# Four-layer graph network on one core: the convolutions' running sums as a tree, the ranking's running sums by pairs of tiles

## The chip, the cores and the metric

One core of one Trainium2 chip. The time is device microseconds of one execution of the whole program (three executions of the kernel before are given, and one profiled execution). Engines are named as in the profile: PE (TensorE; PEld its weight loads), DVE (VectorE), ACT (ScalarE), POOL (GpSimd), SP (SyncE).

## What is computed

12,500 nodes with 64 features, 200,000 edges sorted by their target `dst`. Four layers run in turn, each added to x and normalised per row:

```python
out0 = segment_sum(exp(-w)[:, None] * x[dst], src)            # sums by the edge's source
h1   = [seg_sum, seg_max, seg_mean](edge_attr_32, src), u     # then a two-layer MLP
conv: h = x @ W; out = segment_sum(h[src] * norm, dst) + b    # twice (c1, c2)
attention: softmax of scores over the edges of one dst, out = segment_sum(h[src] * attn, dst)
x = layernorm(x + layer(x))                                   # after each layer
```

What matters here is the segment sum over sorted edges. The kernel makes it as a running sum: state[t] = same_dst[t] * state[t-1] + row[t], where same_dst[t] is 1 if edge t has the target of edge t-1 and 0 otherwise. The state at a node's last edge is its sum.

## The kernel before, in words

The edges are padded to 128 partitions of L = 1568 consecutive edges. One "tile" is one edge of each partition (128 rows), and J = 16 tiles make a block; there are NBLK = 98 blocks. The program has these stages, one after the other.

1. *Preparation and histograms*: ids to digits, one-hot matrices (L1055, L1056), counts on PE.
2. *Ranking*: every edge's place in an order by source is worked out, and a row (message, edge attributes, id) is written there. DVE works block by block: `stage_a(n, q)` does four tiles of block n, each with one step of the running sum of node rows (L1110, into `xb`, which waits by the semaphore v_tiles for the step before) and one rank count (L1112, accumulating into `rank_blk`); `stage_b(n-1, q)` does four selections from PSUM for the block before (L1125, waits for "counted" from PE). Four such rounds make a block; then `positions(n-1)` (L1136, L1137) makes the indices, and `onehots_of(n+1)` (L1092, L1093) the next one-hots. PE makes histograms (L841) and counts (L850), ACT copies and scales rows (L753, behind v_tiles), POOL writes the 16 tiles of a block to HBM by 16 indirect DMAs (L591), behind `positions` of that block.
3. *Source pass*: running sums and maxima over rows sorted by source (L1215, L1220), no gathers.
4. *Dense parts* of a layer: transposes and products on PE, norms on DVE.
5. *Convolution* `conv(g)`, twice (c1 and c2): POOL gathers a block's 16 tiles from a table in HBM by 16 indirect DMAs (L641) into one of four buffers `gb`; it may start block n when DVE has finished block n-4. DVE makes the running sum over the 16 tiles of a block, one instruction for each (L1495), each waiting by the semaphore "chain" for the one before. SP writes the block's states to HBM (L507).
6. *Attention* ("at"): the same gathers, of 68 columns. Its running sum is a tree already: `sums_of` (`join`, L1425) takes 33 instructions per block with waits at the levels alone, and ten more DVE instructions per block deal with the scores. The products of same_dst over 2, 4 and 8 tiles that the tree needs stand in `run`, which lies in the buffers of the digits hi_dst, lo_dst and hi_src and is made ahead of conv("c1") (L1526, L1528).

After each pass POOL fetches the states at the nodes' last edges (L610).

Of the kernel before, what the change touches and what calls it, by code (L numbers as in the profile page):

```python
# [15 lines left out]
P = 128  # L16
# [3 lines left out]
J = 16  # L20
Q = 4
NB = -(-N_EDGES // (P * 2 * J))
L = NB * 2 * J
# [32 lines left out]
    "onehots": 2 * NB, "onehots_used": 2 * NB, "flag": 1, "flagrow": 1, "chain": (J - 1) * NBLK,  # L56
# [91 lines left out]
def program(nc, a, out):  # L148
    with ExitStack() as ctx:
# [104 lines left out]
        def carve(tensor, parts, dt=f32):  # L254

            at, got = 0, {}
            for name, size in parts:
# [7 lines left out]
                              ("junk", (2 + Q) * P // 2), ("hi0", J * P // 2), ("hi1", J * P // 2)])  # L265
# [6 lines left out]
        junk = [cut["junk"].bitcast(bf16)[:, q * P:(q + 1) * P] for q in range(2 + Q)]  # L272
# [27 lines left out]
        def one(onehot, k):  # L300
# [14 lines left out]
               for level, (o, w) in ((1, ("dst", "hi")), (2, ("dst", "lo")), (3, ("src", "hi")))}  # L315
        a16 = [late[f"a16_{h}"] for h in range(2)]
# [396 lines left out]
        def _(act):  # L713
# [29 lines left out]
            for n in range(NBLK):  # L743
# [218 lines left out]
        def _(v):  # L962
# [134 lines left out]
            onehots_of(0)  # L1097
            v.wait_ge(s("decay_ready"), 1)
# [3 lines left out]
            def stage_a(n, q):  # L1102

                h = n % 2
                for k in range(q * Q, (q + 1) * Q):
                    t = n * J + k
                    old = xb[h][:, k - 1, :] if k else xb[1 - h][:, J - 1, :] if n else first_row[:, :]
                    if t:
                        v.wait_ge(s("v_tiles"), t)
                    v.scalar_tensor_tensor(out=xb[h][:, k, :], in0=old, scalar=same_dst[:, t:t + 1],  # L1110
                                           in1=xs[h][:, k, :], op0=ALU.mult, op1=ALU.add).then_inc(s("v_tiles"), 1)
                    rank = v.scalar_tensor_tensor(out=junk[t % 2], in0=ids_in[h][:, k * P:(k + 1) * P],  # L1112
                                                  scalar=src_f[:, t:t + 1], in1=before[:, :],
                                                  op0=ALU.is_equal, op1=ALU.mult, accum_out=rank_blk[:, h, k:k + 1])
                if q == J // Q - 1:
                    rank.then_inc(s("ranked"), 1)

            def stage_b(n, q):

                v.wait_ge(s("counted"), n * (J // Q) + q + 1)  # L1120
                h, group = n % 2, n * (J // Q) + q
                if group:
                    v.wait_ge(s("selected"), group)
# [594 lines left out]
```

## Time and profile before

| | us |
|---|---|
| median of 3 executions | 11174.61 (11172.26 to 11193.84) |
| the profiled execution | 11183.53 |
| its span, first to last instruction | 11181.7 |
| ranking, about 490 to 2885 | 2395 |
| convolution c1, gathers and sums, 3850 to 6043 | 2193 |
| convolution c2, gathers and sums, 6223 to 8415 | 2192 |
| attention, 8707 to 10990 | 2283 |

Of the span, POOL is busy 64%, DVE 42%, PE 16%, ACT 10%. A row of the trace gives for a group of instructions its busy time, the mean of one in ns, then "|" and the idle time of its engine just before them, with what ended that idle time: another engine's instruction, a DMA, "issue" (nothing that the profile shows) or "remote" (a releaser that it doesn't know).

### The profile page before, as it was taken

To read this page: it belongs to the slowest core of one execution; us is meant where nothing else is said; L and a number is where in the kernel's file an instruction comes from. 1 tells how busy PE (TensorE), PEld (TensorE's weight loads), DVE (VectorE), ACT (ScalarE), POOL (GpSimd) and SP (SyncE) were. 2 spreads that over 40 slices of the span, in tenths; PEclk is the share of its full clock that TensorE was granted. 3 is DMA by queue.
4 is the path that set the end of the run, shared out by engine and by line. 5 is a ranking of instruction groups with operands and counts; after the bars stand their busy time and mean duration, and the time that the engine had idled before them with its cause. 6 is when DMAs were issued, how large, how long until landed. Compare 5 with 4: busy or idle time off the path is not lost.

```text
span 11181.7 us, 57120 instructions
## 1 busy us (share of the span) xinstructions
PE 1801.6 (16%) x9285; PEld 1516.5 (14%) x9285; DVE 4736.9 (42%) x20005; ACT 1142.1 (10%) x2728; POOL 7106.9 (64%) x6884
## 2 busy tenths in 40 slices
PE   8744444444000400000000000000001000000000
PEld 7633333333000300000000000000000000000000
DVE  8855555555797422222221222222224344444446
ACT  0143434343000100000000000000000000000000
POOL 0566666666201377777776677777777776666766
PEclk7755555555555555555555555555555555555555
DMA  5144444444575111111111111111111222222221
GB/s 224 57 129 122 129 124 126 124 127 122 204 273 203 32 50 46 48 46 48 46 48 37 50 46 48 46 48 46 48 46 30 54 53 58 53 58 55 56 55 44
DMA packets 570444, 911.29 MB, mean 81 GB/s; under 512 B 333435, under 2 KB 348228, under 8 KB 544824
## 3 DMA queue, kind: packets, MB, share of 16 engines
q1 hardware_dynamic: 350264, 652.74, 17.3%
q0 software_dynamic: 219904, 255.88, 10.8%
q14 instruction: 226, 1.85, 0.1%
q8 instruction: 50, 0.82, 0.0%
HBM read 494.12 MB, written 414.02 MB: 81 GB/s over the span
## 4 chain that ended last, share of the span: by engine, by line
DVE 34%; issue 28%; another core or an unknown queue 17%; POOL 16%; PE 3%; DMA 1%; ACT 1%; DVEq 0%; SPq 0%; POOLq 0%; ACTq 0%
DVE arena_a L1495 16%; POOL arena_a L641 15%; DVE arena_b L1112 4%; DVE arena_a L1110 3%; DVE arena_b L1125 3%; DVE arena_a L1425 3%; POOL arena_a L610 2%; PE bank L811 2%; DVE arena_b L1056 1%; DVE arena_b L1093 1%; PE bank L916 1%; DVE arena_a L1625 0%; PE bank L890 0%; DMA arena_a<-in_a 0%
## 5 line engine op out<-in xcount | busy, mean ns | idle before, releaser
L641 POOL DMA_INDIRECT arena_a<-table_c,decay x3136 | 3284.6, 1047 | 1257.6 <-issue 1051.2
L1495 DVE SCALAR_TENSOR_TENSOR arena_a<-arena_a,same_dst 128x64 f32<-128x64 f32 x3134 | 891.5, 284 | 3449.5 <-DVE arena_a L1495 2713.2
L591 POOL DMA_INDIRECT by_src<-arena_b,idx_blk x1568 | 1570.8, 1002 | 885.8 <-issue 449.4
L641 POOL DMA_INDIRECT arena_a<-table_at,decay x1568 | 1556.8, 993 | 703.8 <-issue 468.4
L1110 DVE SCALAR_TENSOR_TENSOR arena_a<-arena_a,same_dst 128x64 f32<-128x64 f32 x1567 | 441.9, 282 | 711.1 <-remote 547.7
L864 PE MATMUL bank<-ident,chunk_end 128*64 128x128 f32 (+2 forms) x8 | 2.7, 442 | 4416.0 <-DVEq L973 4416.0
L864 PEld LDWEIGHTS bank<-ident,chunk_end 128*64 128x64 f32 (+2 forms) x8 | 1.4, 240 | 4416.6 <-DVEq L973 4416.6
L1112 DVE SCALAR_TENSOR_TENSOR arena_b<-arena_a,src_f,before 128x128 bf16<-128x128 f32 x1568 | 543.7, 347 | 37.4 <-issue 37.4
L850 PE MATMUL bank<-hrows 98*128 98x128 f32 x1568 | 404.0, 440 | 659.5 <-DVE arena_b L1125 331.9
L850 PE MATMUL bank<-hrows,arena_a 98*128 98x128 f32 x1568 | 403.3, 438 | 658.0 <-DVE arena_b L1125 347.4
L753 ACT ACTIVATE arena_b<-arena_a,decay 128x64 f32<-128x64 f32 x1568 | 394.2, 334 | 972.5 <-remote 610.2
L1215 DVE SCALAR_TENSOR_TENSOR arena_a<-arena_a,mask_blk,hrows 128x96 f32<-128x96 f32 x1567 | 489.5, 312 | 7.4 <-DVE arena_a L1220 4.4
L850 PEld LDWEIGHTS bank<-hrows 98*128 98x128 f32 x1568 | 348.7, 327 | 711.6 <-DVE arena_b L1125 313.8
L850 PEld LDWEIGHTS bank<-hrows,arena_a 98*128 98x128 f32 x1568 | 347.3, 326 | 710.6 <-DVE arena_b L1125 329.6
L1125 DVE SCALAR_TENSOR_TENSOR arena_b<-bank,arena_b 128x128 bf16<-128x128 f32 x1568 | 380.7, 287 | 107.9 <-issue 107.1
L599 POOL DMA_INDIRECT fix_rows<-states_src,fix_from_src x1 | 1.0, 957 | 668.3 <-DMA states_src<-arena_a 668.3
L811 PE MATMUL bank<-arena_b 128*98 128x128 bf16 x3136 | 406.5, 299 | 26.9 <-DVE arena_b L1056 24.9
L943 PE MATMUL bank<-ident,arena_a 128*128 128x128 f32 x196 | 67.4, 447 | 2124.3 <-DMA arena_a<-in_a 1141.4
L1220 DVE SCALAR_TENSOR_TENSOR arena_a<-arena_a,cap_blk,hrows 128x32 f32<-128x32 f32 x1567 | 384.8, 246 | 0.0
L811 PEld LDWEIGHTS bank<-arena_b 128*98 128x98 bf16 x3136 | 365.0, 174 | 68.9 <-DVE arena_b L1056 68.6
L571 POOL DMA_INDIRECT x_at_start<-x,start_i x98 | 143.4, 1464 | 276.3 <-DVEq L973 246.7
L943 PEld LDWEIGHTS bank<-ident,arena_a 128*128 128x128 f32 x196 | 28.7, 205 | 2137.2 <-DMA arena_a<-in_a 1148.7
(279 smaller groups left out, 4845.9 us busy)
## 6 DMA issues: line engine op xcount, KB each, us to landing
arena_a<-ids_rows SPq DMA_DIRECT2D x98, 1024.0 KB
states_src<-arena_a SPq DMA_DIRECT2D x98, 1024.0 KB
states_c<-arena_a SPq DMA_DIRECT2D x196, 512.0 KB
hrows<-by_src SPq DMA_DIRECT2D x98, 776.0 KB, 6.1
states_at<-arena_a SPq DMA_DIRECT2D x98, 576.0 KB
x_at_start<-arena_a SPq DMA_DIRECT2D x7, 7168.0 KB, 49.0
arena_a<-x_at_start SPq DMA_DIRECT2D x98, 512.0 KB
arena_a<-table_c,decay POOLq DMA_INDIRECT x3136
```

Of the source, the lines that this page charges most:

```text
L591: pool.indirect_dma_start(out=by_src, out_offset=AT(ap=idx_blk[r][:, k:k + 1], axis=0), in_=rows[r][:, k, :], in_offset=None)\
L641: pool.indirect_dma_start(out=gb[r][:, k * w:(k + 1) * w], out_offset=None, in_=table[g], in_offset=AT(ap=src_i[:, n * J + k:n * J + k + 1 ...
L753: ins = act.activation(rows[n % R][:, k, 0:D], xb[n % 2][:, k, :], ACT.Copy, scale=decay[:, t:t + 1])
L811: last = pe.matmul(hist[k % streams], one(oh_hi[h], k), one(oh_lo[h], k), start=False, stop=False)
L850: last = pe.matmul(p_cnt[q][:, k % Q * P:(k % Q + 1) * P], hi_t[h][:, at], snap[h][:, at], start=True, stop=True)
L1110: v.scalar_tensor_tensor(out=xb[h][:, k, :], in0=old, scalar=same_dst[:, t:t + 1], in1=xs[h][:, k, :], op0=ALU.mult, op1=ALU.add).then_inc ...
L1112: rank = v.scalar_tensor_tensor(out=junk[t % 2], in0=ids_in[h][:, k * P:(k + 1) * P], scalar=src_f[:, t:t + 1], in1=before[:, :], op0=ALU. ...
L1125: chosen = v.scalar_tensor_tensor(out=junk[2 + k % Q], in0=p_cnt[q][:, k % Q * P:(k % Q + 1) * P], scalar=1.0, in1=one(oh_lo[h], k), op0=A ...
L1215: xk = c2.done(v.scalar_tensor_tensor(out=new[:, 0:WS], in0=old[:, 0:WS], scalar=mask_blk[:, q, k:k + 1], in1=tb[h][:, k, 0:WS], op0=ALU.m ...
L1220: ins = v.scalar_tensor_tensor(out=new[:, WS:W01], in0=old[:, WS:W01], scalar=cap_blk[:, q, k:k + 1], in1=tb[h][:, k, D:WS], op0=ALU.min, ...
L1425: return v.scalar_tensor_tensor(out=made[:, k, :], in0=old, scalar=scalar, in1=raw[:, k, :] if first else made[:, k, :], op0=ALU.mult, op1 ...
L1495: ins = v.scalar_tensor_tensor(out=st[h][:, k * D:(k + 1) * D], in0=old, scalar=same_dst[:, e:e + 1], in1=gb[r][:, k * D:(k + 1) * D], op0 ...
```

## The change

Three parts.

*Convolution.* The block's running sum becomes the tree of the attention stage, without its halves: `join(0)` from the carried state, seven joins of raw pairs (k = 3, 5, ..., 15), `join(1)`, then for spans 2, 4 and 8 eight joins each. One semaphore increment stands at the end of each level. That is 33 instructions in place of 16.

*Ranking.* The running sum goes by pairs of tiles: `pair_alone` adds the first tile of a pair to the second; `pair_joined` adds the carried state to the second, by the product `both_same` of the pair's two masks, and then to the first. That is 24 instructions per block in place of 16. Two selections of the block before, and then two rank counts, stand between one pair and the next. ACT waits for pairs (v_pairs). Two more scratch rows ("junk") are there.

*Once*: `both_same` is made by one DVE multiplication, in the buffer hi_dst.

```diff
+    "onehots": 2 * NB, "onehots_used": 2 * NB, "flag": 1, "flagrow": 1, "chain": 4 * NBLK,
...
+        both_same = digits["dst", "hi"][:, :].bitcast(f32)[:, 0:L // 2]
...
-                        act.wait_ge(s("v_tiles"), t + Q)
+                        act.wait_ge(s("v_pairs"), (t + Q) // 2)
...
+            link(v.tensor_tensor(both_same, masks[:, :, 0], masks[:, :, 1], ALU.mult))
...
+            def pair_alone(n, i):
+                h, t = n % 2, n * J + 2 * i
+                ins = v.scalar_tensor_tensor(out=xb[h][:, 2 * i + 1, :], in0=xs[h][:, 2 * i, :],
+                                             scalar=same_dst[:, t + 1:t + 2], in1=xs[h][:, 2 * i + 1, :],
+                                             op0=ALU.mult, op1=ALU.add)
+                if i == 0:
+                    ins.then_inc(s("pair_begun"), 1)
+            def pair_joined(n, i):
+                h, t, pair = n % 2, n * J + 2 * i, n * (J // 2) + i
+                old = xb[h][:, 2 * i - 1, :] if i else xb[1 - h][:, J - 1, :] if n else first_row[:, :]
+                if pair:
+                    v.wait_ge(s("v_pairs"), pair)
+                v.scalar_tensor_tensor(out=xb[h][:, 2 * i + 1, :], in0=old, scalar=both_same[:, pair:pair + 1],
+                                       in1=xb[h][:, 2 * i + 1, :], op0=ALU.mult, op1=ALU.add)
+                v.scalar_tensor_tensor(out=xb[h][:, 2 * i, :], in0=old, scalar=same_dst[:, t:t + 1],
+                                       in1=xs[h][:, 2 * i, :], op0=ALU.mult, op1=ALU.add).then_inc(s("v_pairs"), 1)
...
-                for q in range(J // Q):
+                if n < NBLK:
+                    pair_alone(n, 0)
+                for i in range(J // 2):
+                    if n < NBLK and i + 1 < J // 2:
+                        pair_alone(n, i + 1)
+                    if n:
+                        select(n - 1, 2 * i)
+                        select(n - 1, 2 * i + 1)
                     if n < NBLK:
-                        stage_a(n, q)
-                    if n:
-                        stage_b(n - 1, q)
+                        if i == 0:
+                            v.wait_ge(s("pair_begun"), n + 1)
+                        pair_joined(n, i)
+                        rank_of(n, 2 * i)
+                        rank_of(n, 2 * i + 1)
...
-                    for k in range(J):
-                        if k:
-                            old = st[h][:, (k - 1) * D:k * D]
-                            v.wait_ge(s("chain"), chained)
...
+                    join(0, carried, same_dst[:, e:e + 1], raw[:, 0, :])
+                    for k in range(3, J, 2):
+                        last = join(k, raw[:, k - 1, :], same_dst[:, e + k:e + k + 1], raw[:, k, :])
+                    last.then_inc(s("chain"), 1)
+                    chained += 1
+                    v.wait_ge(s("chain"), chained)
+                    join(1, made[:, 0, :], same_dst[:, e + 1:e + 2], raw[:, 1, :]).then_inc(s("chain"), 1)
+                    chained += 1
+                    for span, product in run.items():
+                        v.wait_ge(s("chain"), chained)
+                        for k in range(J):
+                            if k // span % 2:
+                                last = join(k, made[:, k // span * span - 1, :],
+                                            product[:, n, k // (2 * span) * span + k % span:][:, 0:1],
+                                            raw[:, k, :] if k % span == 0 else made[:, k, :])
+                        if 2 * span < J:
+                            last.then_inc(s("chain"), 1)
                             chained += 1
+                    last.then_inc(s("state"), 1)
```

On DVE, one block of a convolution was this before (same_dst is the mask, arena_a the buffers and the states):

```order
L1495 SCALAR_TENSOR_TENSOR arena_a<-arena_a,same_dst 128x64 [waits gathered2,state,stored0]
L1495 SCALAR_TENSOR_TENSOR arena_a<-arena_a,same_dst 128x64 [waits chain] x15
```

and is this now (hi_dst, lo_dst and hi_src hold the products over 2, 4 and 8 tiles):

```order
L1519 SCALAR_TENSOR_TENSOR arena_a<-arena_a,same_dst 128x64 [waits gathered2,state,stored0]
L1519 SCALAR_TENSOR_TENSOR arena_a<-arena_a,same_dst 128x64 x7
L1519 SCALAR_TENSOR_TENSOR arena_a<-arena_a,same_dst 128x64 [waits chain]
L1519 SCALAR_TENSOR_TENSOR arena_a<-arena_a,hi_dst 128x64 [waits chain]
L1519 SCALAR_TENSOR_TENSOR arena_a<-arena_a,hi_dst 128x64 x7
L1519 SCALAR_TENSOR_TENSOR arena_a<-arena_a,lo_dst 128x64 [waits chain]
L1519 SCALAR_TENSOR_TENSOR arena_a<-arena_a,lo_dst 128x64 x7
L1519 SCALAR_TENSOR_TENSOR arena_a<-arena_a,hi_src 128x64 [waits chain]
L1519 SCALAR_TENSOR_TENSOR arena_a<-arena_a,hi_src 128x64 x7
```

Fifteen waits on "chain" became four, and 16 instructions 33. On DVE in the ranking, a round of four tiles was this before, four times in a block:

```order
L1110 SCALAR_TENSOR_TENSOR arena_a<-arena_a,same_dst 128x64 [waits v_tiles]
L1112 SCALAR_TENSOR_TENSOR arena_b,rank_blk<-arena_a,src_f,before 128x128
L1110 SCALAR_TENSOR_TENSOR arena_a<-arena_a,same_dst 128x64 [waits v_tiles]
L1112 SCALAR_TENSOR_TENSOR arena_b,rank_blk<-arena_a,src_f,before 128x128
L1125 SCALAR_TENSOR_TENSOR arena_b,sel_blk<-bank,arena_b 128x128 [waits selected,counted]
L1125 SCALAR_TENSOR_TENSOR arena_b,sel_blk<-bank,arena_b 128x128 x3
```

(of the four tiles, two stand here), and four tiles are this now:

```order
L1108 SCALAR_TENSOR_TENSOR arena_a<-arena_a,same_dst 128x64
L1141 SCALAR_TENSOR_TENSOR arena_b,sel_blk<-bank,arena_b 128x128 x2
L1120 SCALAR_TENSOR_TENSOR arena_a<-arena_a,hi_dst 128x64 [waits v_pairs]
L1122 SCALAR_TENSOR_TENSOR arena_a<-arena_a,same_dst 128x64
L1128 SCALAR_TENSOR_TENSOR arena_b,rank_blk<-arena_a,src_f,before 128x128 x2
L1108 SCALAR_TENSOR_TENSOR arena_a<-arena_a,same_dst 128x64
L1141 SCALAR_TENSOR_TENSOR arena_b,sel_blk<-bank,arena_b 128x128 [waits selected,counted]
L1141 SCALAR_TENSOR_TENSOR arena_b,sel_blk<-bank,arena_b 128x128
L1120 SCALAR_TENSOR_TENSOR arena_a<-arena_a,hi_dst 128x64 [waits v_pairs]
L1122 SCALAR_TENSOR_TENSOR arena_a<-arena_a,same_dst 128x64
L1128 SCALAR_TENSOR_TENSOR arena_b,rank_blk<-arena_a,src_f,before 128x128 x2
```

With the two instructions of `positions` and the two of `onehots_of`, a block of the ranking had 52 DVE instructions and has 60. Nothing is moved on PE, ACT, POOL or SP.

## Rows read from the trace of the kernel before

**Rows 1.** Busy time by stretch: ranking, c1, attention (stretch, us, PE, PEld, DVE, ACT, POOL)
```profile
490.00:2885.00 2395.00, 1012.35 (x4704) 879.05 (x4704) 1368.43 (x8238) 968.91 (x2158) 1570.83 (x1568) 0.50 0.42 124
3850.00:6070.00 2220.00, 1.37 (x4) 0.79 (x4) 451.06 (x1583) 0.00 (x0) 1658.15 (x1585) 0.50 0.18 47
...
8707.00:10990.00 2283.00, 173.26 (x596) 120.63 (x596) 1000.10 (x4235) 98.77 (x395) 1557.78 (x1569) 0.50 0.24 57
```
**Rows 2.** Groups by line in c1, 3860 to 6044
```profile
L641 POOL DMA_INDIRECT arena_a<-table_c,decay x1560 | 1634.7, 1048 | 523.7 <-issue 523.7
L1495 DVE SCALAR_TENSOR_TENSOR arena_a<-arena_a,same_dst 128x64 f32<-128x64 f32 x1567 | 445.7, 284 | 1725.0 <-DVE arena_a L1495 1363.0 <-remote 158.5 <-issue 108.6
```
**Rows 3.** Timeline of the start of c1 (start us, us, engine line)
```profile
3850.06 1.03 POOL L641 DMA_INDIRECT arena_a<-table_c,decay  x1 [158.94 <-DMA table_c<-hrows]
...
3871.78 4.78 DVE L1495 SCALAR_TENSOR_TENSOR arena_a<-arena_a,same_dst 128x64 f32<-128x64 f32 x15
...
3891.59 5.10 DVE L1495 SCALAR_TENSOR_TENSOR arena_a<-arena_a,same_dst 128x64 f32<-128x64 f32 x16 [15.03 <-DMA arena_a<-table_c,decay]
...
3893.96 0.98 POOL L641 DMA_INDIRECT arena_a<-table_c,decay  x1 [0.30 <-issue]
```
**Rows 4.** Timeline in the middle of c1
```profile
5000.09 1.10 POOL L641 DMA_INDIRECT arena_a<-table_c,decay  x1 [0.30 <-issue]
5000.50 0.28 DVE L1495 SCALAR_TENSOR_TENSOR arena_a<-arena_a,same_dst 128x64 f32<-128x64 f32 x1 [1.11 <-DVE arena_a L1495]
5001.49 1.09 POOL L641 DMA_INDIRECT arena_a<-table_c,decay  x1 [0.30 <-issue]
5001.90 0.28 DVE L1495 SCALAR_TENSOR_TENSOR arena_a<-arena_a,same_dst 128x64 f32<-128x64 f32 x1 [1.12 <-DVE arena_a L1495]
```
**Rows 5.** Timeline of the end of c1
```profile
6017.27 1.09 POOL L641 DMA_INDIRECT arena_a<-table_c,decay  x1 [0.30 <-issue]
...
6041.48 0.28 DVE L1495 SCALAR_TENSOR_TENSOR arena_a<-arena_a,same_dst 128x64 f32<-128x64 f32 x1 [1.81 <-remote]
6042.18 0.28 DVE L1495 SCALAR_TENSOR_TENSOR arena_a<-arena_a,same_dst 128x64 f32<-128x64 f32 x1 [0.41 <-DVE arena_a L1495]
```
**Rows 6.** Group of the gathers in the attention stage
```profile
L641 POOL DMA_INDIRECT arena_a<-table_at,decay x1568 | 1556.8, 993 | 703.8 <-issue 468.4 <-DVE arena_a L1425 160.6 <-remote 74.8
```
**Rows 7.** Timeline in the attention stage
```profile
9458.07 0.29 DVE L1425 SCALAR_TENSOR_TENSOR arena_a<-arena_a,hi_dst 128x68 f32<-128x68 f32 x1 [1.57 <-issue]
...
9459.47 0.29 DVE L1425 SCALAR_TENSOR_TENSOR arena_a<-arena_a,hi_dst 128x68 f32<-128x68 f32 x1 [1.11 <-issue]
...
9465.40 0.94 POOL L641 DMA_INDIRECT arena_a<-table_at,decay  x1 [0.30 <-issue]
...
9468.62 0.97 DVE L1425 SCALAR_TENSOR_TENSOR arena_a<-arena_a,lo_dst 128x68 f32<-128x68 f32 x4 [2.53 <-remote]
...
9473.94 0.94 POOL L641 DMA_INDIRECT arena_a<-table_at,decay  x1 [7.59 <-DVE arena_a L1425]
```
**Rows 8.** Timeline of a block of the ranking
```profile
1600.87 1.44 POOL L591 DMA_INDIRECT by_src<-arena_b,idx_blk  x1 [3.62 <-DVE idx_blk L1137]
...
1602.53 0.28 DVE L1110 SCALAR_TENSOR_TENSOR arena_a<-arena_a,same_dst 128x64 f32<-128x64 f32 x1
...
1603.00 0.28 DVE L1110 SCALAR_TENSOR_TENSOR arena_a<-arena_a,same_dst 128x64 f32<-128x64 f32 x1
...
1619.09 0.28 DVE L1110 SCALAR_TENSOR_TENSOR arena_a<-arena_a,same_dst 128x64 f32<-128x64 f32 x1 [2.26 <-remote]
...
1620.51 0.95 POOL L591 DMA_INDIRECT by_src<-arena_b,idx_blk  x1 [0.30 <-issue]
1621.88 0.28 DVE L1110 SCALAR_TENSOR_TENSOR arena_a<-arena_a,same_dst 128x64 f32<-128x64 f32 x1 [2.24 <-remote]
...
1625.04 1.44 POOL L591 DMA_INDIRECT by_src<-arena_b,idx_blk  x1 [3.58 <-DVE idx_blk L1137]
```
**Rows 9.** What POOL waits for in the ranking, 536 to 2885 (us in total, times, longest)
```profile
POOL by_src L591 <- DVE idx_blk L1137: 350.4, 96, 5.1
```

More of the change, by code:

```diff
@@ L271, in program @@
         rows = [cut[f"rows{r}"].rearrange("p (j f) -> p j f", f=TW) for r in range(R)]
[L272 removed]
+        junk = [cut["junk"].bitcast(bf16)[:, q * P:(q + 1) * P] for q in range(4 + Q)]
         hi_in = [cut[f"hi{h}"].bitcast(bf16)[0:HIGH, :] for h in range(2)]
@@ L1097, in _ @@
             onehots_of(0)
+            masks = same_dst[:, :].rearrange("p (m two) -> p m two", two=2)
+            link(v.tensor_tensor(both_same, masks[:, :, 0], masks[:, :, 1], ALU.mult))
             v.wait_ge(s("decay_ready"), 1)
             v.wait_ge(s("first_row_in"), 16)
[L1102 to L1115, printed above, removed]
-                    rank.then_inc(s("ranked"), 1)
@@ L1118, in stage_b @@
[L1118 to L1123, printed above, removed]
-                for k in range(q * Q, (q + 1) * Q):
-                    chosen = v.scalar_tensor_tensor(out=junk[2 + k % Q], in0=p_cnt[q][:, k % Q * P:(k % Q + 1) * P],
-                                                    scalar=1.0, in1=one(oh_lo[h], k), op0=ALU.mult, op1=ALU.mult,
-                                                    accum_out=sel_blk[:, h, k:k + 1])
-                chosen.then_inc(s("selected"), 1)
+            def pair_alone(n, i):
[5 more added lines that the diff above has]
+                    ins.then_inc(s("pair_begun"), 1)
@@ new lines, in rank_of, with select @@
+            def rank_of(n, k):
+                h, t = n % 2, n * J + k
+                rank = v.scalar_tensor_tensor(out=junk[2 + Q + k % 2 if k % 4 > 1 else k % 2], in0=ids_in[h][:, k * P:(k + 1) * P],
+                                              scalar=src_f[:, t:t + 1], in1=before[:, :],
+                                              op0=ALU.is_equal, op1=ALU.mult, accum_out=rank_blk[:, h, k:k + 1])
+                if k == J - 1:
+                    rank.then_inc(s("ranked"), 1)
+            def select(n, k):
+                q, h, group = k // Q, n % 2, n * (J // Q) + k // Q
+                if k % Q == 0:
+                    v.wait_ge(s("counted"), group + 1)
+                    if group:
+                        v.wait_ge(s("selected"), group)
+                chosen = v.scalar_tensor_tensor(out=junk[2 + k % Q], in0=p_cnt[q][:, k % Q * P:(k % Q + 1) * P],
+                                                scalar=1.0, in1=one(oh_lo[h], k), op0=ALU.mult, op1=ALU.mult,
+                                                accum_out=sel_blk[:, h, k:k + 1])
+                if k % Q == Q - 1:
+                    chosen.then_inc(s("selected"), 1)
@@ new lines, in conv, with join @@
+                    made = st[h][:, 0:J * D].rearrange("p (j c) -> p j c", c=D)
+                    carried = chunk_end[:, 0:D] if n == 0 else st[1 - h][:, (J - 1) * D:J * D]
+                    e = n * J
+                    def join(k, old, scalar, new):
+                        return v.scalar_tensor_tensor(out=made[:, k, :], in0=old, scalar=scalar, in1=new,
+                                                      op0=ALU.mult, op1=ALU.add)
+                    join(0, carried, same_dst[:, e:e + 1], raw[:, 0, :])
```

16 lines of the change are left out of this document (2 added, 14 removed).

## The prediction, on record before the changed kernel's times were seen

> **What bounds the kernel now.** First the busy time by stretch: the two convolutions take 2192 us each (c1 from 3850.06 to 6042.46 [rows 3, 5], c2 as long), the ranking 2395, attention 2283, and in all of them POOL is the busiest engine, with 1560 to 1660 us, though nowhere full [rows 1]. So the question in each is what keeps POOL from its pace. That pace is a gather of 0.94 us and 0.30 us of issue, 1.25 us together, 20.0 us for the 16 of a block, seen in attention beside DVE's work [rows 7] and in c1's first blocks, which start 20 us apart [rows 3].
>
> In c1 the groups by line show that POOL never waits for DVE there (all its idle time is "issue"), yet its mean gather is 1.05 us [rows 2]. The timeline says how: at first DVE does the 16 steps of a block in 5.1 us, 0.32 us a step, chain waits included, and then idles 15 us for the gathers [rows 3]. In the middle of c1 the same step comes every 1.40 us, and POOL's gathers, now 1.09 us long, also every 1.40 us, in lockstep [rows 4]: 16 x 1.40 = 22.4 us a block. The rows say that 1.11 us of each step is a wait for the step before. The first blocks deny it: the same wait cost 0.04 us there. And in attention, joins that wait for nothing also come 1.40 us apart, with no named releaser [rows 7]. So I read the 1.40 us as a **slow mode of DVE, priced per instruction**, not as the latency of a semaphore.
>
> When is DVE slow? In attention POOL's last gather before a stall ends at 9466.34; at 9468.62 DVE does four joins in 0.97 us, finishes, and frees the buffer at which POOL starts again at 9473.94 [rows 7]. In the ranking POOL stands still 3.6 us in each block, then DVE does a tile in 0.47 us, and later in the block, with POOL writing, in 2.8 us, two instructions at 1.40 [rows 8]. In both a standstill of POOL buys DVE a stretch of fast work. c1's end speaks against too simple a rule: POOL's last gather ends at 6018.36 and DVE still makes two steps in 2.8 us at 6042 [rows 5], after 2168 us in which POOL never stood.
>
> **Prices.** I count DVE's instructions per block (attention 43, ranking 52, convolution 16) and give 1 per 1.40 us to the time in which POOL works. Attention: a block is 2283 / 98 = 23.3 us, of it POOL waits (160.6 + 74.8) / 98 = 2.4 us for DVE [rows 1, 6]. In the other 20.9 us go 14.9 instructions, so 28.1 are bought by 2.4 us: 11.7 per us of standstill. Ranking: a block is 24.2 us (1600.87 to 1625.04 [rows 8]), POOL waits 350.4 / 96 = 3.65 us [rows 9], 14.7 go in the other 20.6 us and 37.3 are bought: 10.2 per us. Two stages with different work give nearly the same price; that is why I trust it.
>
> **The convolutions.** 15 waits become 4, and 16 instructions 33. By this reading the waits are worth nothing and the 17 instructions are the cost. What is gained is another thing: with 33 instructions DVE falls behind, POOL runs into its four buffers, stands, and the lockstep breaks as in attention. POOL's gathers then cost 20.0 us a block plus something for DVE's work beside them. Attention's mean of 993 ns would give 16 x (0.993 + 0.30) = 20.7, but it holds a 1.2 us product that c1 lacks; c1's own first blocks, with DVE's steps beside the gather, show 0.98 at most [rows 3], so 20.1. In it go 14.4 instructions; 18.6 remain, at 11.7 to 10.2 per us 1.6 to 1.8 us. Several blocks' debt is paid in one longer stall, so I take 1.5. A block is 21.6 us. For c1: 98 x 21.6 = 2117 for POOL, and a tail of 12 us for DVE's last block (24 before, in slow mode [rows 5]; 7 if all fast): 2129 against 2192, **-63 us, for both -126**. Bounds of the block: 20.1 (no stall; -210 each) and attention's whole 23.3 (+103 each).
>
> One rule of the Trainium skill bears on the step: "VectorE: DVE Perf Modes", Rules for kernel authors, says to minimise the number of operations and not of semaphores, since each operation drains anyway. By that rule the tree, with twice the instructions and fewer waits, brings nothing of itself; the trace agrees (0.32 us with the wait, at first [rows 3], against 0.20 to 0.25 for a join without one [rows 7]), and it speaks against this change.
>
> **The ranking.** The running sum goes from 16 to 24 instructions, a block from 52 to 60. The waits on v_tiles go, but in the fast stretch the tile of 0.47 us is just the two instructions back to back [rows 8], so their going is worth 0. Of the order nothing else is on a path: ACT scales after pairs as it did after tiles, POOL waits for `positions` at the end of the block as before, SP's next loads wait for the last rank count, now the block's last sum, and are wanted a block later. PE's counts for a group wait for the same selections. So 8 instructions more, in front of `positions`, for which POOL waits. At 10.2 per us: 0.8 us a block, +77. Least: DVE is still slow 0.4 us after POOL's last write ended (1621.88 against 1621.46), so all 37 were bought in a good us, and 8 more cost 0.2 us, +20. Most: all 8 behind each other at 0.20 us in POOL's standstill, 1.6 us, +157. I take 0.5, **+50 us**. `both_same` once is under 1 us. The attention stage, the dense parts and the source pass are left as they are: 0.
>
> **Sum.** -126 + 50 = -76 us against the profiled execution's 11183.5, that is 11107; the median of the runs lies 9 us lower, so 11098, say **11100 us**.
>
> **Rivals.**
> *A. The convolutions become like attention or worse (slower).* The mechanism: in slow mode 33 instructions last 46 us against POOL's 20, and if the standstills don't buy DVE a fast stretch soon enough, POOL waits longer than the lockstep cost. For: attention, the same tree on the same gathers, takes 23.3 us a block, more than c1's 22.1 (2168 / 98); and the end of c1, where DVE stayed slow for 24 us without POOL [rows 5]. Against: attention has ten instructions more. It decides from a block of 22.1 us, that is a stall over 2.0 us. At 23.3: 98 x 23.3 + 12 = 2295, +103 each; with the ranking +256, **11430**. Were POOL's gathers to stay at 1.40 us as well, 22.4 + 1.5 = 23.9 would give the same and a little more. Chance 0.20.
> *B. The slow mode is the wait after all, and POOL is the bound.* Then the tree hides: 33 joins of 0.20 us are 7 us, a block is 20.1, 98 x 20.1 + 10 = 1980, -212 each, -374 with the ranking, **10800**. For: the releaser named in rows 2 and 4. Against: rows 3 and 7. Chance 0.13.
> The skill's "Runtime: NRT & Kernel Launch", Instruction fetch mechanics, holds that the supply of instructions is hidden behind their issue; by that rule no price per instruction of 1.40 us could exist, and B would hold. The joins of rows 7, without waits, speak against it; no run so far shows what the 1.40 us is.
> *C. The two parts cancel.* The ranking at its upper price (+157) and the convolutions at 21.5 to 21.6 (-126 to -140): about **11190**. Chance 0.12.
> *D. POOL keeps 1.40 us by itself, whatever DVE does*, its stalls hidden: convolutions as before, ranking +50: **11225**. Against: the early blocks of c1. Chance 0.06.
>
> **Chances.** The forecast, with a gain of 20 to 200 us, has 0.49. A measurement here tells 0.2%, 22 us, from no change. Faster by more: most of the forecast (0.47) and B (0.13), 0.60. Same: C, and the rest of the forecast, 0.14. Slower: A and D, 0.26. The range must hold 0.8: it leaves out B's end and the far half of A: 10870 to 11330. The forecast alone would span 10980 to 11160.
>
> **What would show it.** In c1 after: POOL's mean gather near 0.95 to 0.99 us in place of 1.05, and, new, waits of POOL for the join line, some 150 us in all per convolution, in about 20 stalls of 5 to 10 us; blocks of DVE in 7 us right after a stall and in 40 us and more later; a mean block of 21.6. In the ranking: POOL's wait for the indices 4.1 us a block in place of 3.65, and the v_pairs waits empty. Wrong it would be if POOL waits for nothing and its gathers are 0.94 (B), if its stalls sum to over 200 us per convolution (A), or if the ranking's block grows by over 1 us, or shrinks: a shorter block with 8 more instructions would refute the price per instruction.

## The result, and the profile after

| | before | changed |
|---|---|---|
| median of the runs | 11182.24 us (4) | 11364.18 us (4, 11356.18 to 11385.17) |
| ratio | | 1.0162, 95% interval 1.0145 to 1.0180 |
| span of the profiled execution | 11181.7 us | 11362.8 us |

The change is slower by 182 us, where a gain of 76 was forecast. The busy time by stretch of the changed kernel (ranking, c1, attention; columns: us, PE, PEld, DVE, ACT, POOL), to be read beside [rows 1]:

```profile
490.00:2991.00 2501.00, 1013.98 (x4706) 879.58 (x4704) 1561.11 (x9022) 981.59 (x2158) 1564.17 (x1568) 0.50 0.41 119
3959.00:6190.00 2231.00, 1.37 (x4) 0.79 (x4) 687.60 (x3250) 0.00 (x0) 1498.35 (x1571) 0.50 0.18 46
...
8870.00:11130.00 2260.00, 169.25 (x582) 117.67 (x582) 964.01 (x4081) 96.58 (x385) 1565.33 (x1574) 0.50 0.23 56
```

POOL's 1568 gathers or scatters mark each stage in the same way in both traces, so I measure a stage from the start of the first to the end of the last of them; the tables below all do.

| POOL's stage | before | changed | difference |
|---|---|---|---|
| up to the first scatter | 511.8 | 516.5 | +5 |
| ranking | 2370.6 | 2474.5 | +104 |
| to the first gather of c1 | 967.6 | 968.6 | +1 |
| c1 | 2168.3 | 2205.2 | +37 |
| between | 204.3 | 195.4 | -9 |
| c2 | 2167.8 | 2199.0 | +31 |
| between | 316.7 | 318.4 | +2 |
| attention, and the rest | 2474.5 | 2485.3 | +11 |

Up to rounding they add up to the 181 us between the spans. The attention stage was not changed, and it and the rest took 2476.6 to 2488.7 us in four other kernels at the same level of time (those of the table below), so the 11 us lie within its scatter. What is to be explained is the ranking's +104 and the convolutions' +68.

The group of the gathers in c1, 3959 to 6190 (busy, mean ns | idle time before, releasers), and what POOL waits for in the ranking (us in total, times, longest):

```profile
L642 POOL DMA_INDIRECT arena_a<-table_c,decay x1568 | 1496.1, 954 | 867.8 <-issue 471.6 <-DMA table_c<-hrows 158.8 <-remote 121.0
```
```profile
POOL by_src L592 <- DVE idx_blk L1154: 458.6, 95, 5.5
```

Beside [rows 2] the mean gather went from 1048 to 954 ns, so the lockstep is gone, as forecast. But new waits took more than it had cost: POOL stands 22 times in c1 for over 2.5 us, 235 us in all, and a cycle of five blocks is 112.5 us nearly throughout. In the ranking the wait for the indices went from 3.65 us a block [rows 9] to 4.83.

The timeline of a slow stretch of c1 in the changed kernel (start us, us, engine line):

```profile
4395.77 1.69 DVE L1519 SCALAR_TENSOR_TENSOR arena_a<-arena_a,lo_dst 128x64 f32<-128x64 f32 x8 [8.85 <-remote]
4396.02 0.95 POOL L642 DMA_INDIRECT arena_a<-table_c,decay  x1 [0.30 <-issue]
...
4406.97 1.26 DVE L1519 SCALAR_TENSOR_TENSOR arena_a<-arena_a,hi_src 128x64 f32<-128x64 f32 x6 [9.51 <-remote]
```

Here the 1.40 us shows a face that the kernel before could not show. VectorE runs the eight joins of a level back to back in 1.69 us. Then the wait for the last of them takes 9.5 us, so levels start 11.20 us apart, and that is 8 x 1.40. So within a level it is not the start of the instructions that comes at one per 1.40 us; I read it as their being reported done. The trace shows only when the wait returns. And this is how one of POOL's standstills goes:

```profile
4442.37 0.95 POOL L642 DMA_INDIRECT arena_a<-table_c,decay  x1 [0.30 <-issue]
4451.07 1.66 DVE L1519 SCALAR_TENSOR_TENSOR arena_a<-arena_a,hi_src 128x64 f32<-128x64 f32 x8 [7.43 <-remote]
4455.32 2.01 DVE L1519 SCALAR_TENSOR_TENSOR arena_a<-arena_a,same_dst 128x64 f32<-128x64 f32 x9 [2.60 <-issue]
...
4455.50 0.95 POOL L642 DMA_INDIRECT arena_a<-table_c,decay  x1 [12.18 <-remote]
```

POOL stops at 4443.32 just as a level has been issued; that level's wait lasts to 4451.07, the next to 4455.3, and only then is VectorE fast. In attention it was fast 2.3 us after POOL stopped [rows 7].

### The profile page after: what moved, and what is told of

The parts are those of the page before. It is cut to its first block and busy times, and to the rows that moved or that the text cites. A ratio compares the mean times of both kernels' runs of the same rounds, so it can differ in the third digit from the quotient of the medians.

```text
span 11362.8 us, 61334 instructions
## 1 busy us (share of the span) xinstructions
PE 1803.4 (16%) x9285; PEld 1517.1 (13%) x9285; DVE 5400.8 (48%) x24122; ACT 1154.9 (10%) x2728; POOL 6808.2 (60%) x6884
## 3 DMA queue, kind: packets, MB, share of 16 engines
q0 software_dynamic: 219904, 255.88, 10.7%
## 5 line engine op out<-in xcount | busy, mean ns | idle before, releaser
L642 POOL DMA_INDIRECT arena_a<-table_c,decay x3136 | 2992.6, 954 | 1616.9 <-issue 941.7
L1519 DVE SCALAR_TENSOR_TENSOR arena_a<-arena_a,same_dst 128x64 f32<-128x64 f32 x1762 | 385.7, 281 | 1416.6 <-issue 812.5
L1519 DVE SCALAR_TENSOR_TENSOR arena_a<-arena_a,lo_dst 128x64 f32<-128x64 f32 x1568 | 326.2, 281 | 824.4 <-remote 696.7
L1519 DVE SCALAR_TENSOR_TENSOR arena_a<-arena_a,hi_src 128x64 f32<-128x64 f32 x1568 | 325.2, 281 | 727.8 <-remote 634.7
L1128 DVE SCALAR_TENSOR_TENSOR arena_b<-arena_a,src_f,before 128x128 bf16<-128x128 f32 x1568 | 500.6, 349 | 147.1 <-issue 146.2
L1141 DVE SCALAR_TENSOR_TENSOR arena_b<-bank,arena_b 128x128 bf16<-128x128 f32 x1568 | 406.2, 289 | 184.1 <-issue 183.7
L812 PE MATMUL bank<-arena_b 128*98 128x128 bf16 x3136 | 406.8, 299 | 26.7 <-DVE arena_b L1057 23.3
L1519 DVE SCALAR_TENSOR_TENSOR arena_a<-arena_a,hi_dst 128x64 f32<-128x64 f32 x1568 | 326.0, 281 | 72.4 <-DVE arena_a L1519 49.3
```

What stands on the lines that cost most here:

```text
L642: pool.indirect_dma_start(out=gb[r][:, k * w:(k + 1) * w], out_offset=None, in_=table[g], in_offset=AT(ap=src_i[:, n * J + k:n * J + k + 1 ...
L812: last = pe.matmul(hist[k % streams], one(oh_hi[h], k), one(oh_lo[h], k), start=False, stop=False)
L1128: rank = v.scalar_tensor_tensor(out=junk[2 + Q + k % 2 if k % 4 > 1 else k % 2], in0=ids_in[h][:, k * P:(k + 1) * P], scalar=src_f[:, t:t ...
L1141: chosen = v.scalar_tensor_tensor(out=junk[2 + k % Q], in0=p_cnt[q][:, k % Q * P:(k % Q + 1) * P], scalar=1.0, in1=one(oh_lo[h], k), op0=A ...
L1519: return v.scalar_tensor_tensor(out=made[:, k, :], in0=old, scalar=scalar, in1=new, op0=ALU.mult, op1=ALU.add)
```

## The experiments

The experiments were run in groups, each on one chip and together with the kernel before. In eight of nine groups the kernel before took 10079 to 10102 us instead of 11182 to 11195. The steps of 1.40 us were absent there in every stage, and one chip showed them in one group and not in another. I say "mode on" and "mode off" of this. Every ratio is to the kernel before in the same group, with a 95% interval, and stages are compared only between runs of the same mode. Which mode a group met could not be chosen. The code below is shortened: "..." and calls with arguments left out stand for the rest.

**The parts alone** (mode off). `e1_convs` takes the diff's convolutions alone, `e2_rank` its ranking alone.

> Only the convolutions are changed (33 VectorE instructions per block in a tree), the ranking is that of before. Theory A (the stages add up, as the two traces have it: c1 +36.9 us, c2 +31.2, the stretches around them -8, the rest of the attention stage up to +20): 11240 to 11270 us beside about 11182 before, POOL standing about 10.7 us every five blocks as in the changed kernel. Theory B (the loss comes from the ranking alone, and the longer convolutions are an effect of the state that the ranking leaves behind): 11182 or less.

> Only the ranking is changed (60 instructions per block, selections and rank counts between), the convolutions are those of before. Theory A (stages add up): the ranking 2474 us from first to last scatter, +104, and the total 11285 to 11310. Theory B (the ranking's loss is an effect of something else): under 11230.

Measured: 1.0020 (1.0011 to 1.0030) and 0.9988 (0.9978 to 0.9998). With the mode off POOL's idle time between two gathers or scatters of a stage is nowhere over 0.3 us. `e1_convs`: c1 1970 us. `e2_rank`: ranking 2043, c1 1960. Neither theory could be tested as it was meant; what came out is that the loss needs the mode. So the changed kernel itself was run:

> The changed kernel as it is, where the kernel before takes 10088 us. Theory M (the whole loss of 182 us belongs to the mode in which VectorE's instructions pass at one per 1.40 us, which the last four runs did not show: no POOL standstill over 2.3 us in any stage): within 20 us of the kernel before on this chip, 10085 to 10110, the sum of the two parts run alone (+20, -12). Theory X (part of the loss is in the dependencies of the new ranking and tree themselves): 10150 or more. Should this run be one with the mode of 1.40 us, both expect 11364 beside 11182, and it tells nothing between them.

Measured (mode off, one run each): 10099.6 us beside 10080.5, theory M. This is the tree in that run:

```profile
4394.99 1.78 DVE L1519 SCALAR_TENSOR_TENSOR arena_a<-arena_a,same_dst 128x64 f32<-128x64 f32 x8
4396.81 1.66 DVE L1519 SCALAR_TENSOR_TENSOR arena_a<-arena_a,hi_dst 128x64 f32<-128x64 f32 x8
4398.50 1.66 DVE L1519 SCALAR_TENSOR_TENSOR arena_a<-arena_a,lo_dst 128x64 f32<-128x64 f32 x8
4400.19 1.66 DVE L1519 SCALAR_TENSOR_TENSOR arena_a<-arena_a,hi_src 128x64 f32<-128x64 f32 x8
4414.66 0.48 DVE L1519 SCALAR_TENSOR_TENSOR arena_a<-arena_a,same_dst 128x64 f32<-128x64 f32 x2 [12.81 <-DMA arena_a<-table_c,decay]
```

A level's wait is 0.03 us, and VectorE idles 12.8 us for data. Same kernel, same instructions: nearly the whole of the 182 us belongs to the mode.

**The order of the ranking** (mode off). `e3_order` keeps the 16 joins in a chain but takes the new order:

```diff
-    for q in range(J // Q):      # four (join, rank), then four selections
-        stage_a(n, q); stage_b(n - 1, q)
+    for i in range(J // 2):
+        select(n - 1, 2 * i); select(n - 1, 2 * i + 1)
+        for k in (2 * i, 2 * i + 1):
+            join(n, k); rank_of(n, k)
```

> The ranking keeps its running sum of 16 instructions (52 instructions per block, as before) but takes the new order: two selections, then two joins with a rank count behind each. Theory N (the number of VectorE instructions is the price, 8 more per block for +104 us, order free): ranking stage 2350 to 2395 us, total 11160 to 11210. Theory O (the order is the price: selections spread over the block hold up the joins and so the scaling, the next counts and the indices): ranking 2440 to 2480 us, total 11250 to 11300.

Measured: 1.0040 (1.0026 to 1.0054), the ranking 2094 us beside 2048 and 2051 with the old order in the same group. The theories were about the mode and stay untested; but with 16 joins in a chain the new order has a price even where VectorE is not what POOL waits for:

```profile
L591 POOL DMA_INDIRECT by_src<-arena_b,idx_blk x1568 | 1616.6, 1031 | 563.4 <-issue 477.1 <-DVE idx_blk L1140 85.7 <-ACT arena_b L753 0.6
```

It comes through POOL's scatters, 1031 ns instead of 1001 to 1003; 28 to 30 ns times 1568 are the 45 us. It is not the order alone: `e2_rank` has the same order with joins by pairs, its scatters take 998 ns and its ranking 2043 us. Why they are longer in `e3_order` I did not find.

**Fewer, wider instructions** (mode off). In `e4_wide` a level of the tree is a product and a sum over 512 elements (shown against the tree of the changed kernel), ten instructions per block in all:

```diff
-    join(k, made[:, k // span * span - 1, :], product[...], ...)    # eight per level
+    v.tensor_tensor(tmp, last_of_first_half.to_broadcast(...), masks.to_broadcast(...), ALU.mult)
+    v.tensor_tensor(second_half, new, tmp, ALU.add)
```

> The convolutions' tree in whole levels: per block one join, one copy of 7 rows and 8 instructions of 512 elements (a product with the masks spread over the channels, then a sum), 10 instructions with 8 waits for the engine's own signal, instead of 16 with 15 (before) or 33 with 4 (the change). Ranking as before. Theory N (each VectorE instruction costs 1.40 us while POOL issues, whatever it waits for): 10 or 11 times 1.40 = 15.4 us per block, under POOL's 20.1, so POOL never waits: c1 and c2 1970 us each instead of 2168, total 10780 to 10810. Theory W (a wait for the engine's own signal costs about 10 us while POOL works, as between the levels of the changed kernel): 80 us per block, c1 and c2 far above 2500 us, total above 12000. Theory P (POOL's 1.40 us per gather comes back whenever VectorE's instructions have a wait each): 22.4 us per block, total 11180.

Measured: 1.0117 (1.0100 to 1.0134), c1 2018 us. A case that I had not foreseen, slower for another reason: the gathers beside it.

```profile
L641 POOL DMA_INDIRECT arena_a<-table_c,decay x1568 | 1540.6, 983 | 549.6 <-issue 477.5 <-DMA table_c<-hrows 72.0
```

With the 16 joins in a chain the same group has a mean of 946 ns (`e2_rank`), with 33 joins 952 (`e1_convs`). Each wide instruction is busy 0.69 us, and 37 ns more on each of 16 gathers are 0.6 us a block, 58 us a convolution, and that is the whole difference in c1 (2018 against 1960).

**Four kernels with the mode on** (one group, the kernel before at 11194.54 us; the rows "before" and "changed" of the table are from the traces above).

`e6_pairs`, convolutions in 24 instructions (pairs without waits, then eight steps of two):

```diff
+    for k in range(1, J, 2): join(k, raw[k - 1], same_dst[e + k], raw[k])
+    for i in range(J // 2):
+        join(2 * i + 1, old, both[pair], made[2 * i + 1]).then_inc(chain)
+        join(2 * i, old, same_dst[e + 2 * i], raw[2 * i]); wait(chain)
```

> Convolutions by pairs as in the new ranking: 24 VectorE instructions per block (8 pair joins without waits, then 8 times two with a wait each), ranking as before. Where VectorE runs free (no 1.40 us mode), theory M (VectorE's work is hidden behind POOL's gathers): c1 and c2 1960 to 1970 us each, total within 20 us of the kernel before. Where the 1.40 us mode is on: theory N (a number of instructions is what counts, a standstill of some 10.7 us is due for each 80 instructions too many): 25 times 98 less 1400 in 1967 us is 1050 too many, 13 standstills, c1 2110 us, the total 110 us under before. Theory W (waits count): like before, 2168.

`e7_grouped`, the ranking by pairs in the old grouping, convolutions as before:

```diff
-    select(n - 1, 2 * i); select(n - 1, 2 * i + 1)      # between the joins
+    for k in range(q * Q, (q + 1) * Q): select(n - 1, k)  # after each four tiles
```

> The ranking by pairs (60 instructions) in the old grouping: four tiles' joins and rank counts, then four selections together; convolutions as before. Without the 1.40 us mode: theory O (the place of the selections matters to POOL's own pace, as the run with only the new order had 1.031 us per scatter instead of 1.00): 2040 to 2055 us with the selections together; theory I (the order doesn't matter, that run's loss had another cause): the same as the run with only the ranking changed, 2043, within 5. With the mode: theory N (8 instructions more are the loss) 2475 us as in the changed kernel; theory O 2370 to 2400.

`e8_signals`, the change's tree with a signal and a wait for each instruction:

> The change's tree of 33 instructions with a signal and a wait for it at every instruction instead of at every level. Without the mode: VectorE needs 33 times 0.32 = 10.6 us of each 20.1 us block, so c1 and c2 1965 to 1975 us as with the tree alone (1970, 1969), total within 10 of it. With the mode: theory L (the wait behind a level of eight is what makes POOL's standstills 12 us long): shorter standstills and c1 under 2180 us; theory N alone: 2205 as in the changed kernel; theory W (each wait costs): above 2300.

`e9_wide2`, convolutions in 13 instructions (wide product and sum for the pairs, a chain of eight, one, wide product and sum):

> Convolutions by pairs in 13 instructions: two of 512 elements, eight joins in a chain, one join, two of 448 elements; VectorE busy some 4.5 us per block instead of about 6 in the first wide kernel and 4.5 with 16 joins. Without the mode: theory B (POOL's gathers are slowed by the time that VectorE spends in wide instructions, 0.983 us instead of 0.946 with 10 of them): between, 0.955 to 0.975 us per gather and c1 1975 to 2005 us; theory C (slowed by the reads with masks spread over the channels, or by something per instruction): outside of that. With the mode: 14 times 1.40 is 19.6 us per block, under POOL's 20.1 to 20.6: c1 1970 to 2030 us, total 10800 to 10910 beside 11182.

| mode on | per block | total, ratio | ranking | c1 | c2 | POOL's standstills in c1 | mean gather in c1 |
|---|---|---|---|---|---|---|---|
| before | 16, 15 waits | | 2370.6 | 2168.3 | 2167.8 | 0 | 1047 ns |
| changed | 33, 4 waits | 1.0162 | 2474.5 | 2205.2 | 2199.0 | 22, 235 us | 954 |
| `e6_pairs` | 24, 8 waits | 1.0027 (1.0016 to 1.0039) | 2366.4 | 2197.3 | 2188.5 | 29, 237 us | 950 |
| `e7_grouped` | ranking 60 | 1.0122 (1.0093 to 1.0151) | 2504.0 | 2168.4 | 2167.9 | 0 | 1048 |
| `e8_signals` | 33, 32 waits | 1.0190 (1.0160 to 1.0220) | 2372.8 | 2265.4 | 2262.2 | 34, 302 us | 951 |
| `e9_wide2` | 13, 11 waits | 1.0002 (0.9991 to 1.0013) | 2369.9 | 2168.4 | 2168.0 | 0 | 1078 |

The standstills counted are those over 2.5 us. What follows, one by one. The stages add up: with the ranking alone changed (`e7_grouped`) the convolutions are those of before within 0.1 us, with the convolutions alone changed (`e8_signals`) the ranking is within 2.2 us. (The change's own convolutions without its ranking were not run with the mode on.) Nine instructions fewer per block gave no shorter standstills: 237 us with 24, 235 us with 33. My theory N, a standstill due for so many instructions too many, is refuted by that (c1 2110 expected), and `e7_grouped`, at 2504 us, fits neither of its theories (2475, or 2370 to 2400). And `e9_wide2`, which was expected to gain 140 to 200 us a convolution, ties with the kernel before. Its gathers (from the groups of c1), and one block of its timeline:

```profile
L641 POOL DMA_INDIRECT arena_a<-table_c,decay x1568 | 1689.8, 1078 | 639.2 <-issue 478.6 <-DMA table_c<-hrows 160.6
```
```profile
4409.59 0.69 DVE L1511 TENSOR_TENSOR arena_a<-arena_a,same_dst 128x512 f32<-128x512 f32 x1 [17.02 <-DMA arena_a<-table_c,decay]
...
4411.24 2.53 DVE L1495 SCALAR_TENSOR_TENSOR arena_a<-arena_a 128x64 f32<-128x64 f32 x8
...
4414.47 0.63 DVE L1520 TENSOR_TENSOR arena_a<-arena_a 128x448 f32<-128x448 f32 x1
4415.19 1.10 POOL L641 DMA_INDIRECT arena_a<-table_c,decay  x1 [0.30 <-issue]
...
4416.59 1.09 POOL L641 DMA_INDIRECT arena_a<-table_c,decay  x1 [0.30 <-issue]
4417.99 1.79 POOL L641 DMA_INDIRECT arena_a<-table_c,decay  x1 [0.31 <-issue]
4420.09 1.10 POOL L641 DMA_INDIRECT arena_a<-table_c,decay  x1 [0.30 <-issue]
4421.49 1.10 POOL L641 DMA_INDIRECT arena_a<-table_c,decay  x1 [0.30 <-issue]
4422.89 0.94 POOL L641 DMA_INDIRECT arena_a<-table_c,decay  x1 [0.30 <-issue]
...
4431.91 0.69 DVE L1511 TENSOR_TENSOR arena_a<-arena_a,same_dst 128x512 f32<-128x512 f32 x1 [16.82 <-DMA arena_a<-table_c,decay]
```

This block decides the convolutions. VectorE is not slow at all: its eight chained steps take 2.53 us, 0.32 us each as with the mode off, it is done in 5.5 us and idles 17 us for the gathers. POOL waits for nothing. Yet the block takes 22.32 us and the next 22.5, because eight of POOL's gathers come 1.40 us or more after the one before, six of them when VectorE is done. The first 13 blocks of that c1 take 20.2 to 20.5 us each, then the pace is 22.40 us on average to the end, the same 22.40 as in the kernel before after its first 11 blocks of 20.0 [rows 3, 4]. The wide instructions are not the reason: the 13 early blocks have the same ones. Nor is it one supply that the two engines share, an instruction of either each 0.70 us (32 in 22.4 us in the kernel before): 16 gathers and 13 instructions would be due in 20.3 us.

The trace of the kernel before shows the same from the other side. Its VectorE takes 5.1 us for each of the first three blocks of c1, then 5.8, 8.2, 10.7 and so on, and 20.4 us for the tenth, while POOL's blocks still take 20.0 us. VectorE is slow first, and POOL follows its own pace until its twelfth block. In `e9_wide2`, with 13 instructions per block, VectorE is fast throughout c1.

**One instruction per block, and the ranking in fewer** (mode off, nine runs). `e10_bare` replaces a block's sums in both convolutions by one copy of its rows, so it leaves the running sums out:

```diff
-    for k in range(J): ... v.scalar_tensor_tensor(...)
+    v.tensor_copy(st[h][:, 0:J * D], gb[r][:, 0:J * D]).then_inc(s("state"), 1)
```

> Each block of the two convolutions has one VectorE instruction (a copy of its 16 gathered rows) in place of its sums, so the convolutions' running sums are left out; all else as before. Where the 1.40 us mode is on (the kernel before at about 11190 us): theory F (in this mode POOL itself has a floor of 1.40 us per gather, 22.4 us per block, after a credit of some 26 us, whatever VectorE does): c1 and c2 2168 us each as before, gathers at 1.25 us for the first 11 to 13 blocks and then 22.4 us per block. Theory N (the two engines share one supply, an instruction of either each 0.70 us): 17 or 18 instructions per block, POOL never held, 1965 us each. Where the mode is off, both: 1960.

`e11_select` makes the selections of a group by one product and one reduction, 44 instructions in the ranking's block, and `e12_fewer` adds the message sums in 13, 41 in all:

```diff
-    for k in ...: chosen = v.scalar_tensor_tensor(..., accum_out=sel_blk[:, h, k:k + 1])
+    v.tensor_tensor(picked, p_cnt[q], oh_lo[h][:, q], ALU.mult); wait
+    v.tensor_reduce(sel_blk[:, h, q * Q:(q + 1) * Q], picked, AX.X, ALU.add)
```

> The ranking's 16 selections per block become four products of 512 elements and four reductions (44 VectorE instructions per block instead of 52, VectorE's busy time about the same); all else as before. With the mode on: theory N for the ranking (what matters there is the number of VectorE instructions; the change's eight more gave +104 us, the eight in the old grouping +133): 2240 to 2270 us for the ranking, the total 100 to 130 us under before, 11060 to 11090. Theory F alone (POOL's floor of 22.4 us per block): no less than 2195. Theory D (the dependence of the selections on the counts sets the block, not the number): 2370 as before or more. With the mode off: the ranking within 20 us of 2043.

> As the last one, and the message sums in 13 instructions per block (pairs by two wide instructions, eight joins in a chain, one, two wide), 41 instructions per block in all. With the mode on: theory N: 2195 to 2240 us for the ranking, near POOL's floor, total 11010 to 11060. Theory D: 2370 or more, since the scaling begins only when all sums are made. With the mode off: 2040 to 2080 us.

Measured: 0.9984 (0.9973 to 0.9995), 0.9996 (0.9985 to 1.0008), 0.9987 (0.9975 to 0.9998), with c1 at 1962 us in `e10_bare` and the ranking at 2050 and 2041 us in the others. The mode was off, so they only show that with it off VectorE's work is hidden in every stage, from 1 instruction per block to 33. The first and the last were run again (`e13_bare_again` 0.9987, 0.9976 to 0.9999; `e14_fewer_again` 0.9992, 0.9980 to 1.0003), and one kernel with both questions in it, `e15_both` (its first convolution is without its sums), was run four times over an hour:

> One kernel for both open questions: the ranking in 41 VectorE instructions per block (as in the two runs before), the first convolution with one VectorE instruction per block (its running sums are left out), the second convolution and the attention stage as before. With the 1.40 us mode on: theory F (POOL has a floor of 22.4 us per block of its own): c1 2168 us, as c2; theory N (shared supply): c1 1965, c2 2168. Ranking: 2195 to 2240 us if the number of VectorE instructions sets it, 2370 or more if the dependences do. With the mode off: 2040, 1960, 1960 and 2040 us for the four stages, 10085 in all.

`e15_both` took 10072.85 us beside 10087.76, `e16_both_again` 10072.01 beside 10078.98, `e17_both_third` 10076.55 beside 10095.42, `e18_both_fourth` 0.9977 (0.9965 to 0.9988): the mode was off in all, and the stages came out as expected for that, 2040 to 2044, 1957, 1961 and 2038 to 2039 us. `e12_fewer` computes the same results as the kernel before and was faster by 0.13% in one group and 0.08% in the other, with intervals that reach to 0.02% or across 1; what it does with the mode on was not seen. No version here beats the kernel before by more than such a hair, and of all of them only the changed kernel was timed in both modes.

## Why the prediction was wrong

**"POOL's gathers then cost 20.0 us a block."** True, and not enough. The lockstep did break, the mean gather fell to 954 ns, a block of gathers without a standstill is 16 x 1.25 = 20.1 us. But I took the 2.3 us a block that the lockstep cost for a thing between the two engines that would go with it. `e9_wide2` shows POOL held to 22.40 us a block by something that is neither a wait nor a slow VectorE. Four kernels whose VectorE has 13 to 33 instructions per block and 4 to 15 waits come out at 2168 to 2205 us (`e8_signals`, with 32 waits, at 2265), and in the two of them in which POOL stands still the standstills give back just what the gathers gained: 20.1 + 2.4 = 22.5 in the changed kernel (112.5 us per five blocks), 20.0 + 2.4 in `e6_pairs`. The reading that fits all of them is that with the mode on POOL may issue one gather per 1.40 us in the long run, with a credit of some 26 us at first (11 blocks x 16 x 0.15 us), and that a standstill earns credit. By it no change of VectorE's work could have made a convolution shorter than 2168 us, and the -63 us of each could not exist. This premise, that breaking the lockstep frees POOL, is what failed behind the sum. The reading is rival D, which I gave 0.06 and argued away by "the early blocks of c1"; by it those are the credit. It is inferred from these kernels and not shown; the kernel that tests it directly, one VectorE instruction per block, never met the mode.

In the changed kernel itself, though, POOL never came to the end of that credit. Counted from the starts of its gathers, the furthest that it runs ahead of one per 1.40 us is 14 us, where the kernel before, `e7_grouped` and `e9_wide2` reach 27 us and stay there (`e8_signals` 14, `e6_pairs` 21). So what holds POOL there is its wait for VectorE, and that is a term of the sum:

**"Several blocks' debt is paid in one longer stall, so I take 1.5."** This is the failed step. It was 2.4 us a block, the 235 us: 0.9 us a block more than I took are 88 us of POOL's time in c1 (2205 against 2117). Why it comes so near to what the gathers had gained is open; it is no constant, since in `e8_signals` it is 3.1 us. The 2.4 us are over rival A's point of 2.0 us, and A's sign and mechanism came true at a third of its size (+34 us on average per convolution instead of +103). The stall's start is the part that I had missed: behind a level, VectorE's wait still has up to 8.7 us to go when POOL stops.

**"The waits are worth nothing and the 17 instructions are the cost."** Half right with the mode on. `e8_signals` puts 28 waits more on the same 33 instructions and c1 grows by 60 us, 0.6 us a block, 0.02 us per wait: small, but not nothing. Of the instructions, the nine between 24 and 33 made c1 8 us longer, 0.01 us each, with four waits fewer. With VectorE fast a wait shows too: 0.32 us a step [rows 3] against 0.20 us without one, which I had called agreement. And the expectation that signals at every instruction would shorten the standstills (theory L) fell: 302 us instead of 235, and c1 at 2265 us lies between that expectation's theories (2205, and over 2300).

**The price, 11.7 to 10.2 instructions per us of standstill.** It cannot be a price: 235 and 237 us of standstill went with 33 and 24 instructions. The near agreement of two stages, which made me trust it, was luck.

**"The ranking: I take 0.5, +50 us."** Sign and mechanism hold: 60 instructions instead of 52 made the block 1.06 us longer, all of it POOL's wait for the indices, inside my bounds of +20 and +157. The size was twice what I took: 0.13 us per instruction. In the old grouping the same 60 instructions cost +133 us, 0.17 us each, so the new order gave some 30 us back where I had held "Of the order nothing else is on a path". With the mode off the same order cost 46 us with 16 joins and nothing with pairs (2043 us), so its effect is not one number.

**The rule on instruction fetch.** The Trainium skill's "Runtime: NRT & Kernel Launch", Instruction fetch mechanics, has the supply of instructions hidden behind their issue. With the mode off the trace agrees: joins come every 0.20 us, 1.66 us for eight. With it on they do as well within a level of the convolutions: of 2600 instructions without a wait in the changed kernel's c1 none starts 1.35 to 1.45 us after the one before, and what is late is the end of the wait. In a chain the two look the same, so the kernel before could not tell them apart. But late ends of waits do not explain all: in its attention stage 101 joins without a wait start 1.35 to 1.45 us after the one before, among them the one at 9459.47 in [rows 7]. Whether the supply of instructions has a part in those stays open.

**Rival B**, POOL as the bound at 20.1 us a block, is what the runs with the mode off show (20.1 us a block in `e5_after`); but there the chain of 16 is hidden as well, so the change has nothing to gain (1.0020 with the convolutions alone).

**What I said would show it wrong** did: standstills over 200 us per convolution, and a ranking block longer by over 1 us.

**Three small slips.** "0.98 at most" passes over c1's first gather, 1.03 us [rows 3]. Attention's 2283 us hold 23 us behind its last gather; its gathers take 2260, 23.1 us a block and not 23.3. And rival C's parts, +157 with -126 to -140, give 11192 to 11206 and not 11190. None of them moves the forecast by more than a few us.

## What to carry to other kernels

Before pricing a loss by what engine A does to engine B, look for a kernel or a stretch in which A is idle, and see whether B has its pace there; a rate that stays while A idles for three quarters of the block is not made by waiting for A. A pace at the start of a stage that is lost after a fixed amount of work can be a credit being spent; it is no proof of what the engine can keep up. And where one engine's pace is the floor of a stage, another schedule on another engine can add to the time but gains nothing.

## What the runs showed of the hardware that I had not expected

- The same kernel took 10079 to 10102 us in eight groups of runs and 11182 to 11195 in the others, 11% apart. The granted clock does not differ enough to explain it: 0.517 or 0.518 over the faster executions, 0.515 or 0.516 over the slower, and 0.50 through the convolutions of both. With the mode off a convolution is 1960 us instead of 2168, the ranking about 2050 instead of 2371, attention 2037 instead of 2260. One chip showed both at different times. The kernel was the same, so nothing in it sets the mode, and its cause stays open.
- With the mode on, eight independent instructions of VectorE start 0.20 us apart, and in the slow stretches of c1 a wait for the last returns 11.2 us after the first started: 1.40 us for each.
- With it on, where POOL never stands, its gathers settle at 16 per 22.40 us after 11 to 13 blocks at 20.0 to 20.5, also beside a VectorE that idles 17 us of the 22.
- POOL's gathers are longer beside wide VectorE instructions with the mode off: 946 ns with 16 joins of 64 columns per block, 952 with 33, 983 with eight of 512 columns and a copy.
